# Quantising scales from the maxima alone in a cross-attention and FFN kernel, x normalised by add and multiply, and the instruction orders of all five engines laid anew

## The chip, the cores and the metric

The kernel runs on one NeuronCore of a Trainium2 chip. The core has five engines that run their own instruction streams beside each other: TensorE (PE in the profile), VectorE (DVE), ScalarE (ACT), GpSimd (POOL) and SyncE (SP, which here only issues DMAs). They meet at semaphores alone. The metric is the device time of one launch in microseconds (us), as the median of several runs.

## The reference

One layer of top-k cross-attention, then a feed-forward network whose activations are quantised to 8 bits and whose weights are ternary. All tensors are float32; x is 2048x256, the context 1601x256.

```python
def act_quant(x):
    scale = 127.0 / jnp.clip(jnp.max(jnp.abs(x), axis=-1, keepdims=True), 1e-05)
    q = jnp.clip(jnp.round(x * scale), -128.0, 127.0) / scale
    return x + jax.lax.stop_gradient(q - x)

def bitlinear(x, w, b):
    xq = act_quant(rmsnorm(x))
    wq = weight_quant(w)
    return jnp.einsum('bsd,fd->bsf', xq, wq) + b

# attention: q, k, v projected; scores = q k^T / 16; only the 32 largest
# scores of a row are kept (top_k = 32 of 1601); softmax, times v, projected by Wo
x = x + attention(layernorm(x), ctx)
# FFN: 256 -> 1024 -> 256
h = gelu(bitlinear(layernorm(x), w1, b1))
x = x + bitlinear(h, w2, b2)
```

`rmsnorm(x)` is `x * rsqrt(mean(x*x) + 1e-5)`. A row's maximum after rmsnorm is the row's maximum before it times that row's inverse spread r, so in `round(x * r * 127 / max(x * r))` the r cancels, except where the clip at 1e-5 holds. It is left in the factor that takes the integer back.

## The kernel before

**Tiles.** The 2048 rows are 16 tiles of 128 rows, and two tiles are a pair (8 pairs, `j = t // 2`). Set-up turns the context (13 blocks of 128 rows), folds Wq into Wk and Wo into Wv (`fold_queries`, `fold_values`), and projects the keys in four chunks of 400 or 401 columns (`project_keys`) and the values block by block (`project_values`). Scores need float32 accuracy, so each such product is made of high and low parts, three matmuls for one.

**One tile t.** PE: `scores(t, c)` for four chunks, six matmuls each. ACT: `copy_scores` to `s_sb`. DVE: `candidates` (the 8 largest of each piece of 50), `best_8` and three `next_8` (the 32nd largest of all), `count`, `weigh` (mask times exponentials), `largest_count` and `release(t)`, which raises `p_ready`. ACT: `exp_all(t)` after `best_8(t, 0)`. PE after `release(t)`: `turn_weights(t, q)`, 13 transposes in four quads through the two PSUM banks TURN; ACT: `take_weights` (`pT`, L1101) copies each quad out; PE: `weighted(t, q)`, 26 matmuls. DVE: `attended`, `moments`, `centre` give x2, its mean and variance, and `cen_max`.

**The FFN of a pair.** POOL: `row_scales_1` makes the scales in seven dependent steps of two columns, with the inverse spread second (power -0.5) and the quantising scale sixth. `quantise_1` makes y1; PE turns it (`turn_y1`), `up` multiplies by w1; ACT `hidden` scales by the seventh value; POOL `add_bias`; ACT `gelu` and `squares` (the sums for the second spread); DVE `gelu_max`. POOL `row_scales_2` then waits for squares and maxima, seven steps again; ACT `quantise_2` and `lower_2`; SP turns y2 by DMA, PE `down`, DVE `output`, SP `store`. The last two pairs turn y2 on PE (`turn_y2`), and the last pair makes its scales on DVE tile by tile (`tile_scales_1`, `tile_scales_2`, L1530 to L1534, four steps in front of the quantising), with the power -0.5 on POOL (`root_1`, `root_2`).

**Order.** No scheduler and no pool is in play. Each engine's order is the order in which its calls are written: a set-up by hand, a loop over rounds r in which every stage stands at a fixed offset, and an end by hand. PSUM banks are handed out by `fill` in PE's written order, to the bank of a group that was filled longest ago, so PE waits for whoever has still to drain it. `s_sb`, `e_all` and `pT` have two copies: `copy_scores(t)` waits for `release(t - 2)`.

**Around the change.** `normalise_scale` and `normalise` (L755 to L764, POOL) make xn = (x - mean) * r, `split_queries` (L770) the low part of q, for which `scores` waits. `sum_weights` (L1077, ACT) sums the absolute FFN weights and waits for the DMAs of both w1 and w2. `hold_clock(23)` is 23 transposes whose result nobody reads. The lines that make x normal and the first scale are

```python
pool.tensor_scalar(xn[:, u, :], x_in[:, u, :], ln1_mv[:, u, 0:1], ln1_r[:, 1, u:u + 1],
                   ALU.subtract, ALU.mult)
```

## Time and profile before

| | us |
|---|---|
| median of 3 runs | 279.48 (278.39 to 279.64) |
| span of the profiled execution, first to last instruction | 277.2 |
| PE busy | 262.5 (95%) |
| DVE busy | 230.2 (83%) |
| ACT busy | 215.8 (78%) |
| POOL busy | 165.0 (60%) |

Only the span of the profiled execution is given, not a time with what lies around it. Busy time of PE is modelled from overlapping matmuls: one matmul of `weighted` lasts 0.38 us by itself, while they start 0.22 us apart. So the idle time of PE is what is to be read, and it is spread thinly.

### The profile page before, as it was taken

The numbers are of one execution on the slowest core, as the hardware profiler recorded it, in microseconds if no ns is written. First come the engines' busy times: TensorE is split into PE (matmuls) and PEld (weight loads), VectorE is DVE, ScalarE is ACT, GpSimd is POOL, SyncE is SP. The second block draws the span as 40 slices with busy tenths as digits, with TensorE's granted clock in tenths as the row PEclk, the third lists the DMA queues.
The fourth block names the chain that finished last, engine by engine and source line by source line (L and its number), as shares of the span: only waits on it lengthen the run. The fifth ranks groups of instructions, "written<-read, shape, count | busy, mean of one in ns | idle before, by whom it ended". The sixth has DMA issues, their size and how long they took to land. (4 is left out here: it accounts for less than half of the span.)

```text
span 277.2 us, 5366 instructions
## 1 busy us (share of the span) xinstructions
PE 262.5 (95%) x1527; PEld 230.4 (83%) x1527; DVE 230.2 (83%) x984; ACT 215.8 (78%) x323; POOL 165.0 (60%) x235
## 2 busy tenths in 40 slices
PE   7999999999999899999999999999999999799784
PEld 7999998998887788988898889888978898577463
DVE  2561868988979897989898989899989798989894
ACT  2567495586589988988799879987998899647762
POOL 3334409931888587849775887678767943612330
PEclk9999999999999999999999999999999999999999
DMA  6991010046000330025001500151004100610011
GB/s 223 316 342 40 4 38 0 1 79 151 2 2 0 77 78 0 0 69 125 0 4 45 139 5 4 38 140 18 0 1 124 31 1 2 151 38 5 0 38 38
DMA packets 29436, 16.42 MB, mean 59 GB/s; under 512 B 20445, under 2 KB 28190, under 8 KB 29406
## 3 DMA queue, kind: packets, MB, share of 16 engines
q1 hardware_dynamic: 28702, 15.02, 20.3%
q0 software_dynamic: 272, 0.79, 1.0%
q10 hardware_dynamic: 432, 0.26, 0.3%
q8 instruction: 12, 0.20, 0.3%
q14 instruction: 18, 0.15, 0.2%
HBM read 9.77 MB, written 2.10 MB: 43 GB/s over the span
## 5 line engine op out<-in xcount | busy, mean ns | idle before, releaser
L399 PE MATMUL bank<-vo,pT 128*128 128x257 f32 (+1 forms) x416 | 97.1, 381 | 2.4 <-ACT pT L1101 2.4
L399 PEld LDWEIGHTS bank<-vo,pT 128*128 128x128 f32 (+1 forms) x416 | 76.0, 190 | 15.1 <-ACT pT L1101 4.8
L1413 DVE MAX8 cand<-s_sb 128x8 f32<-128x50 f32 (+1 forms) x512 | 60.0, 201 | 1.6 <-issue 1.1
L258 PE MATMUL score<-k_high,q_low 128*128 128x400 f32 (+1 forms) x128 | 49.5, 387 | 0.0
L868 POOL TENSOR_TENSOR g<-g,b_bc 128x512 f32<-128x512 f32 x24 | 37.9, 1592 | 12.1 <-ACT g L1125 12.1
L258 PE MATMUL score<-k_low,q_high 128*128 128x400 f32 (+1 forms) x128 | 44.2, 346 | 0.0
L258 PE MATMUL score<-k_high,q_high 128*128 128x400 f32 (+1 forms) x128 | 44.0, 344 | 0.0
L1052 ACT ACTIVATE s_sb<-score 128x400 f32<-128x400 f32 x64 | 30.6, 504 | 10.2 <-PE score L258 10.1
L1101 ACT ACTIVATE pT<-bank 128x512 f32<-128x512 f32 x64 | 31.9, 514 | 4.2 <-PE bank L266 4.2
L1448 DVE SCALAR_TENSOR_TENSOR e_all<-s_sb,best,e_all 128x1601 f32<-128x1601 f32 x16 | 34.2, 2138 | 0.9 <-ACT e_all L1093 0.5
L266 PE MATMUL bank<-ident,e_all 128*128 128x128 f32 (+1 forms) x208 | 30.7, 273 | 2.6 <-ACT pT L1101 2.6
L1093 ACT ACTIVATE e_all<-s_sb,neg_max 128x1601 f32<-128x1601 f32 x16 | 26.1, 1629 | 4.5 <-DVE neg_max L1426 4.5
L266 PEld LDWEIGHTS bank<-ident,e_all 128*128 128x128 f32 (+1 forms) x208 | 24.4, 140 | 5.6 <-issue 3.6
L764 POOL TENSOR_SCALAR xn<-x_in,ln_mv,ln_r 128x256 f32<-128x256 f32 x16 | 27.8, 1741 | 0.9
L258 PEld LDWEIGHTS score<-k_high,q_low 128*128 128x128 f32 x128 | 24.1, 189 | 2.4
L258 PEld LDWEIGHTS score<-k_low,q_high 128*128 128x128 f32 x128 | 24.2, 189 | 0.7
L258 PEld LDWEIGHTS score<-k_high,q_high 128*128 128x128 f32 x128 | 24.1, 189 | 0.0
L1609 DVE TENSOR_REDUCE g_max<-g 128x1 f32<-128x1024 f32 x14 | 17.0, 1218 | 7.6 <-ACT g L1135 7.6
L1423 DVE MAX8 best<-cand 128x8 f32<-128x64 f32 (+1 forms) x64 | 20.8, 325 | 2.0
L822 POOL TENSOR_SCALAR row<-ln_mv 128x2 f32<-128x2 f32 x7 | 1.3, 192 | 28.8 <-issue 15.4
L1135 ACT ACTIVATE g<-g 128x1024 f32<-128x1024 f32 x14 | 14.9, 1067 | 3.7 <-POOL g L868 3.7
L1125 ACT ACTIVATE g<-bank,row 128x512 f32<-128x512 f32 x24 | 15.8, 685 | 2.3 <-PE bank L430 2.1
(162 smaller groups left out, 503.2 us busy)
## 6 DMA issues: line engine op xcount, KB each, us to landing
x_in<-in_x SPq DMA_DIRECT2D x16, 128.0 KB, 2.2
w_sb<-in_L_ffn_w SPq DMA_DIRECT2D x2, 1024.0 KB, 12.1
x_res<-in_x SPq DMA_DIRECT2D x16, 128.0 KB, 2.9
out<-o_sb SPq DMA_DIRECT2D x16, 128.0 KB, 2.0
ctx_sb<-in_ctx SPq DMA_DIRECT2D x2, 512.0 KB, 7.6
ctx_sb<-in_ctx SPq DMA_DIRECT2D x2, 256.0 KB, 4.1
b_bc<-in_L_ffn_b POOLq DMA_DIRECT2D x1, 512.0 KB, 7.6
w_q<-in_L_xattn_Wq SPq DMA_DIRECT2D x1, 256.0 KB, 2.8
```

Of the source, the lines that this page charges most:

```text
L258: ins = pe.matmul(out, a, b, start=(i == 0), stop=(i == len(steps) - 1))
L266: ins = pe.transpose(bank[0:src.shape[1], at:at + rows], src, ident[0:rows, 0:rows])
L399: ins = pe.matmul(bank[:, 0:DV], pT[0:n, t % 2, b * P:(b + 1) * P], vo[0:n, b, :], start=(b == 0), stop=(b == SB - 1))
L764: pool.tensor_scalar(xn[:, u, :], x_in[:, u, :], ln1_mv[:, u, 0:1], ln1_r[:, 1, u:u + 1], ALU.subtract, ALU.mult).then_inc(xn_ready, 1)
L868: pool.tensor_tensor(g[:, t % 2, part], g[:, t % 2, part], b1_bc[:, part], ALU.add).then_inc(biased, 1)
L1052: act.activation(s_sb[:, t % 2, at:at + n], score[c][:, 0:n], ACT.Copy).then_inc(s_copied, 1)
L1093: act.activation(e_all[:, t % 2, :], s_sb[:, t % 2, :], ACT.Exp, bias=neg_max[:, t % 2:t % 2 + 1], scale=SCALE).then_inc(e_ready, 1)
L1101: drain(act.activation(pT[0:rows, t % 2, lo * P:hi * P], bank(("p", t, q))[0:rows, 0:(hi - lo) * P], ACT.Copy), ("p", t, q))
L1413: ins = dve.max(cand[:, t % 2, k:CAND:PIECES], s_sb[:, t % 2, k * PIECE:end])
L1423: dve.max(best[:, u, k, :], cand[:, u, 0:DEPTH[k] * PIECES]).then_inc(topk_step[u], 1)
L1448: dve.scalar_tensor_tensor(e_all[:, u, :], s_sb[:, u, :], least_kept(t), e_all[:, u, :], ALU.is_ge, ALU.mult).then_inc(masked, 1)
L1609: dve.tensor_reduce(g_max[:, t % 2:t % 2 + 1], g[:, t % 2, :], AX.X, ALU.max, apply_absolute_value=True).then_inc(g_max_ready, 1)
```

## The change

1. **Scales from the maxima alone.** The quantising scale is now 127 over the maximum, in two steps (`scales_1`, `scales_2` on POOL), with clips 1e-5 * EPS and 1e-5 * EPS ** 0.5 in place of 1e-5. The spread, its power -0.5 and the factor back are four steps of their own (`dequant_1`, `dequant_2`), placed elsewhere in the order. `quantise_1` and `quantise_2` wait for the first two steps. `scales_2` waits for the maxima and no more for `squares`. In the last pair `tile_scales_1` is two steps and `tile_scales_2` three on DVE.
2. **x normalised by add and multiply.** The mean is negated first (one more step of two columns) and then added.
3. **Orders.** The loops are gone; every engine has one written list of the same calls. `sum_weights(0)` and `(1)` stand in front of the last key copies on ACT, `weight_mean` in front of the first scores on PE, and `hold_clock(23)` behind the last matmul.

```diff
-                pool.tensor_scalar(xn[:, u, :], x_in[:, u, :], ln1_mv[:, u, 0:1], ln1_r[:, 1, u:u + 1],
-                                   ALU.subtract, ALU.mult).then_inc(xn_ready, 1)
+                pool.tensor_scalar(xn[:, u, :], x_in[:, u, :], ln1_r[:, 2, u:u + 1], ln1_r[:, 1, u:u + 1],
+                                   ALU.add, ALU.mult).then_inc(xn_ready, 1)
...
-            def row_scales_1(j):
+            def scales_1(j):
...
-                shifted, r, z, step_size, inverse, sc, dq = (row1[:, v, k, :] for k in range(7))
-                step(pool.tensor_scalar(shifted, ln2_mv[:, pair, 1], 1.0 + EPS, EPS * EPS, ALU.mult, ALU.add))
-                step(pool.tensor_tensor(r, shifted, minus_half[:, :], ALU.pow))
-                step(pool.tensor_tensor(z, r, cen_max[:, pair], ALU.mult))
-                step(pool.tensor_scalar(step_size, z, 1e-5, 1.0 / 127.0, ALU.max, ALU.mult))
-                step(pool.tensor_tensor(inverse, step_size, minus_one[:, :], ALU.pow))
-                step(pool.tensor_tensor(sc, inverse, r, ALU.mult))
-                pool.tensor_scalar(dq, step_size, wmean[:, 0:1], None, ALU.mult).then_inc(row1_step, 1)
+                pool.tensor_scalar(row1[:, v, 0, :], cen_max[:, pair], CLIP1, 1.0 / 127.0, ALU.max,
+                                   ALU.mult).then_inc(row1_step, 1)
+                pool.wait_ge(row1_step, base + 1)
+                pool.tensor_tensor(row1[:, v, 1, :], row1[:, v, 0, :], minus_one[:, :], ALU.pow).then_inc(row1_step, 1)
...
             def quantise_2(t):
...
-                act.wait_ge(row2_step, j * ROW2 + 6)
+                act.wait_ge(row2_step, j * ROW2 + 2)
...
             down(13)
-            hold_clock(23)
             turn_y2(14, 0)
             turn_y2(14, 1)
             turn_y2(15, 0)
             turn_y2(15, 1)
             down(14)
             down(15)
+            hold_clock(23)
```

**How the order moves, first place: ACT in the set-up.** `ctx_high`, `k_high` and `wvo_high` are copies that PE's next products wait for, `w1T,wsum` is `sum_weights`, `vo` the values, `q_high` and `q_full` the queries. Before:

```order
L1033 ACTIVATE k_high<-bank,k_bias 128x400
L1003 ACTIVATE bvo_bc<-bank 128x256
L1003 ACTIVATE vo<-bank 128x2x256
L1043 ACTIVATE q_high<-bank,ones 128x512
L1044 ACTIVATE q_full<-bank,ones 128x512
L1077 ACTIVATE w1T,wsum<-w_sb 128x2048
L1033 ACTIVATE k_high<-bank,k_bias 128x401
L1052 ACTIVATE s_sb<-score 128x400
L1033 ACTIVATE k_high<-bank,k_bias 128x401
```

After:

```order
L1231 ACTIVATE k_high<-bank,k_bias 128x400
L1222 ACTIVATE ctx_high<-bank 128x2x65
L1276 ACTIVATE w1T,wsum<-w_sb 128x2048
L1231 ACTIVATE k_high<-bank,k_bias 128x400
L1201 ACTIVATE bvo_bc<-bank 128x256
L1231 ACTIVATE k_high<-bank,k_bias 128x400
L1276 ACTIVATE w1T,wsum<-w_sb 128x2048
L1201 ACTIVATE vo<-bank 128x2x256
L1231 ACTIVATE k_high<-bank,k_bias 128x401 x2
```

Both sums have moved ahead of key copies: the first ahead of four, and the second ahead of the last two.

**Second place: ACT towards the end**, after `exp_all(14)`. `y_raised` and `y` are `quantise_2` and `lower_2` of tiles 10 and 11, `pT` of 128x512 a quad of tile 14, `s_sb` a chunk of scores of tile 15. Before:

```order
L1161 ACTIVATE y_raised<-g,magic_col,row 128x1024
L1179 ACTIVATE y<-y_raised,unmagic_col 128x1024
L1052 ACTIVATE s_sb<-score 128x401
L1161 ACTIVATE y_raised<-g,magic_col,row 128x1024
L1179 ACTIVATE y<-y_raised,unmagic_col 128x1024
L1101 ACTIVATE pT<-bank 128x512 x2
L1093 ACTIVATE e_all<-s_sb,neg_max 128x1601
```

After:

```order
L1362 ACTIVATE y_raised<-g,magic_col,row 128x1024
L1301 ACTIVATE pT<-bank 128x512
L1250 ACTIVATE s_sb<-score 128x401
L1301 ACTIVATE pT<-bank 128x512
L1380 ACTIVATE y<-y_raised,unmagic_col 128x1024
L1354 ACTIVATE g_sq,g_ssq<-g 128x1024
L1301 ACTIVATE pT<-bank 128x512
L1293 ACTIVATE e_all<-s_sb,neg_max 128x1601
```

The copies of tile 14's quads have moved ahead of `lower_2(11)`, and a `squares` has moved in behind it.

**Third place: DVE at the very end**, from `hidden(15, 1)` (`s_sb<-score,row,b_bc`) on. `y_raised` is a half of the last quantising, `g_max` a maximum of half a tile. Before:

```order
L1584 SCALAR_TENSOR_TENSOR s_sb<-score,row,b_bc 128x512 x2
L1564 TENSOR_SCALAR row<-g_ssq 128x1
L1632 SCALAR_TENSOR_TENSOR o_sb<-score,row,x2b 128x256
L1592 TENSOR_REDUCE g_max<-s_sb 128x1
L1530 SCALAR_TENSOR_TENSOR row<-g_max,row 128x1
L1531 TENSOR_SCALAR row<-row 128x1
L1532 RECIPROCAL row<-row 128x1
L1533 TENSOR_TENSOR row<-row 128x1
L1534 TENSOR_SCALAR row<-row,wmean 128x1
L1564 TENSOR_SCALAR row<-g_ssq 128x1
L1592 TENSOR_REDUCE g_max<-s_sb 128x1
L1601 TENSOR_SCALAR y_raised<-s_sb,row 128x512
```

After:

```order
L1928 SCALAR_TENSOR_TENSOR s_sb<-score,row,b_bc 128x512
L1945 TENSOR_SCALAR y_raised<-s_sb,row 128x512
L1936 TENSOR_REDUCE g_max<-s_sb 128x1 x2
L1894 TENSOR_SCALAR row<-g_max 128x1
L1897 TENSOR_SCALAR row<-row 128x1
L1899 RECIPROCAL row<-row 128x1
L1906 TENSOR_SCALAR row<-g_ssq 128x1
L1945 TENSOR_SCALAR y_raised<-s_sb,row 128x512
L1976 SCALAR_TENSOR_TENSOR o_sb<-score,row,x2b 128x256
```

The step that waits for the squares (`row<-g_ssq`) stood ahead of the last maximum and now stands behind the scale, tile 14's scales are done before this stretch, and `output(13)` has gone behind the last quantising.

## Rows read from the trace of the kernel before

**Rows 1.** The page, part 1: busy us, share of span, instructions.
```profile
PE 262.5 (95%) x1527; PEld 230.4 (83%) x1527; DVE 230.2 (83%) x984; ACT 215.8 (78%) x323; POOL 165.0 (60%) x235
```

**Rows 2.** Windows: stretch, its us, busy us of PE, PEld, DVE, ACT, POOL, PEclk, DMA.
```profile
0.00:27.50 27.50, 25.93 (x156) 24.98 (x157) 12.00 (x30) 14.42 (x26) 10.34 (x24) 1.00 0.70 232
27.50:50.00 22.50, 22.50 (x147) 21.58 (x146) 18.03 (x103) 15.00 (x26) 11.46 (x10) 1.00 0.05 13
50.00:230.00 180.00, 176.37 (x994) 154.35 (x993) 161.25 (x728) 155.75 (x228) 129.78 (x174) 1.00 0.19 44
230.00:257.00 27.00, 24.42 (x138) 19.74 (x137) 23.22 (x82) 18.87 (x28) 8.94 (x21) 1.00 0.20 50
257.00:277.20 20.20, 13.28 (x100) 9.76 (x97) 15.67 (x43) 11.78 (x18) 4.49 (x8) 0.99 0.08 26
```

**Rows 3.** Waits of PE: line waited, for whom, us, times, longest.
```profile
PE bank L266 <- ACT pT L1101: 3.3, 5, 1.7
PE bank L399 <- ACT pT L1101: 2.4, 5, 0.6
```

**Rows 4.** Timelines of the set-up: start, us, engine, line, operation [idle before].
```profile
6.56 3.13 SPq L662 DMA_DIRECT2D w_sb<-in_L_ffn_w  x1
25.33 1.92 ACT L1077 ACTIVATE w1T<-w_sb 128x2048 bf16<-128x2048 f32 x1
25.59 1.30 POOL L770 TENSOR_TENSOR q_low<-q_full,q_high 128x512 fp32r<-128x512 f32 x1 [2.05 <-ACT q_full L1044]
27.55 0.34 PE L258 MATMUL score<-k_high,q_low 128*128 128x400 f32 x1
30.42 3.69 DVE L1413 MAX8 cand<-s_sb 128x8 f32<-128x50 f32 x32
```

**Rows 5.** The tile w_sb: from issue to landing of its two DMAs.
```profile
DMA to landing us min/median/max: 10.4/12.1/13.8
```

**Rows 6.** Costliest groups: count, busy us, mean ns, idle before.
```profile
L764 POOL TENSOR_SCALAR xn<-x_in,ln_mv,ln_r 128x256 f32<-128x256 f32 x16 | 27.8, 1741 | 0.9
L835 POOL TENSOR_SCALAR y<-cen,row 128x256 f32<-128x256 f32 x14 | 6.5, 479 | 0.7
L1609 DVE TENSOR_REDUCE g_max<-g 128x1 f32<-128x1024 f32 x14 | 17.0, 1218 | 7.6 <-ACT g L1135 7.6
L1161 ACT ACTIVATE y_raised<-g,magic_col,row 128x1024 f32<-128x1024 f32 x14 | 17.3, 1242 | 0.2 <-POOL row L890 0.2
```

**Rows 7.** Timelines of ACT and PE around 237 us.
```profile
235.28 1.23 ACT L1161 ACTIVATE y_raised<-g,magic_col,row 128x1024 f32<-128x1024 f32 x1
236.54 1.15 ACT L1179 ACTIVATE y<-y_raised,unmagic_col 128x1024 bf16<-128x1024 f32 x1
237.60 1.06 ACT L1101 ACTIVATE pT<-bank 128x512 f32<-128x512 f32 x2
238.32 0.63 PE L266 MATMUL bank<-ident,e_all 128*128 128x128 f32 x4 [1.72 <-ACT pT L1101]
```

**Rows 8.** Timeline of DVE behind the last attention product.
```profile
257.05 0.17 DVE L1497 RECIPROCAL inv_sum<-bank 128x1 f32<-128x1 f32 x1 [0.72 <-PE bank L399]
264.71 1.40 DVE L1584 SCALAR_TENSOR_TENSOR s_sb<-score,row,b_bc 128x512 f32<-128x512 f32 x2
268.09 0.67 DVE L1592 TENSOR_REDUCE g_max<-s_sb 128x1 f32<-128x512 f32 x1
269.08 0.69 DVE L1530 SCALAR_TENSOR_TENSOR row<-g_max,row 128x1 f32<-128x1 f32 x1
```

**Rows 9.** Timelines of ACT and PE in the same stretch, and PE's first matmuls.
```profile
266.81 1.06 ACT L1153 ACTIVATE g_sq<-s_sb 128x1024 bf16<-128x1024 f32 x1
270.48 0.82 ACT L1170 ACTIVATE y_raised<-s_sb,magic_col,row 128x512 f32<-128x512 f32 x1 [1.77 <-DVE row L1533]
265.57 2.67 PE L420 MATMUL bank<-ident 128*128 128x128 f32 x23
271.35 1.09 PE L266 MATMUL score<-ident,y_raised 128*128 128x128 f32 x8 [1.47 <-ACT y_raised L1170]
1.52 4.95 PE L462 MATMUL score<-ident 128*128 128x128 f32 x22 [1.52 <-POOL ident L739]
```

More of the change, by code:

```diff
@@ L557, in _ @@
+            down(9)
+            turn_weights(13, 2)
+            weighted(13, 0)
             turn_weights(13, 3)
@@ L945, in _ @@
             quantise_1(2, 1)
[L946 to L976 removed]
+            dequant_1(2)
@@ new lines, in _ @@
+            copy_scores(13, 0)
+            hidden(8, 1)
+            take_weights(11, 0)
+            hidden(9, 0)
+            take_weights(11, 1)
+            copy_scores(13, 1)
+            hidden(9, 1)
+            gelu(8)
+            gelu(9)
+            exp_all(12)
+            take_weights(11, 2)
+            take_weights(11, 3)
+            quantise_2(8)
+            copy_scores(13, 2)
+            lower_2(8)
+            take_weights(12, 0)
+            squares(8)
+            take_weights(12, 1)
@@ new lines, in _ @@
+            copy_scores(13, 3)
+            take_weights(12, 2)
+            squares(9)
+            quantise_2(9)
+            take_weights(12, 3)
+            take_queries(7)
+            exp_all(13)
+            lower_2(9)
+            take_y1(5)
+            copy_scores(14, 0)
+            hidden(10, 0)
+            copy_scores(14, 1)
+            hidden(10, 1)
+            copy_scores(14, 2)
+            hidden(11, 0)
+            copy_scores(14, 3)
+            hidden(11, 1)
+            gelu(10)
@@ L1740, in _ @@
             count(13)
+            output(8)
             attended(12)
```

1331 lines of the change are left out of this document (898 added, 433 removed).

## The prediction, made before the changed kernel had run

> **What bounds the kernel now.** I read the page's first part, then windows by stage, then PE's waits, then timelines where PE idles. PE is busy 262.5 us of 277.2 [rows 1], so its idle time is 14.7 us, and no reordering gives back more than that. The windows say where it lies [rows 2]: 1.6 us up to 27.5, none up to 50, 3.6 in the 180 us from 50 to 230, 2.6 from 230 to 257, and 6.9 in the last 20.2. In the middle the others are close behind: per 180 us DVE is busy 161 and ACT 156. So three engines run at 87 to 98%, and a late copy on ACT or a late mask on DVE reaches PE at once. PE's waits in the attention are all for `pT`, the ACT copies of the turned weights [rows 3]: 3.3 us ahead of transposes and 2.4 ahead of products. The end is another regime: behind the last `weighted` (257.05 [rows 8]) 20.2 us follow in which single steps wait for each other, and of PE's busy time there 2.67 us are `hold_clock` [rows 9].
>
> **Set-up, a loss of 0.7 us for PE and a gain for DVE.** `sum_weights(0)` now stands ahead of the third chunk's key copies. It waits for both FFN weight loads. The second was issued at 6.56 and the slower of the two took 13.8 us [rows 4, 5], so it lands near 20.4; `sum_weights` lasts 1.92, so the first key copy behind it starts near 22.4, while PE, by its own work, has those keys ready near 20.8. Behind it stand two more copies (0.6 each), the second sum (to about 26.2) and `take_values(0)` (to 26.8), which frees the bank that `weight_mean` takes. So the first scores start near 27.0 instead of 27.55 [rows 4]. But PE has less behind it then: `project_values(1)`, 12 matmuls 0.12 apart or 1.4 us, now comes later, `weight_mean` (0.14) earlier. 27.55 - 1.3 = 26.3 would be no loss, so 27.0 is a loss of 0.7. POOL is a second candidate for last: `join_biases` waits for the bias copy (to about 23.5), then 0.7, two `normalise`, and the split of 1.30 [rows 4]. With `normalise` at 0.48 that ends at 26.5, with 1.22 at 28.0, and the loss is then 1.7. DVE, in return, no longer has copies of scores ahead of its last key step; `candidates(0)` starts near 28.8, not 30.42.
>
> **Normalising on POOL.** `(subtract, mult)` on 256 columns lasts 1.74 us in the mean, `(mult, add)` on as many 0.48 [rows 6]. `(add, mult)` with two column operands isn't in the trace. Its bounds are these two rows; I take 0.48, since add and multiply are the two operations of the fast row and subtract is the one thing that only the slow row has. That is 16 x 1.26 = 20 us less of POOL, against 8 small steps of 0.2. POOL is busy 60%, and its `normalise` has almost no one waiting for it (the queries are turned rounds ahead), so on PE's path I count nothing for it in the middle, from either bound. The cover is the distance of the queries; if it is gone, one late `normalise` costs 1.2. The Trainium skill ("GPSIMD Engine Reference", 3.1 Elementwise) has every body of up to two operations at 1.03 cycles an element, which makes 256 columns about 0.4 us by an estimate from that page, whatever the operations. The row of 0.48 agrees, the row of 1.74 does not, so the trace and not the page says that subtract is dear.
>
> **Scales from the maxima.** For the first six pairs the quantising scale waits for two POOL steps instead of six, and the second no more for `squares`. `quantise_2` waits 0.2 us for it in 14 instructions today [rows 6]: there is nothing to gain where it stands. What the split buys is freedom of place, and the new order spends it by quantising sooner after the gelu. The dequant steps are out of the way of `quantise_1` but `hidden` waits for them now; between them lie `turn_y1`, its copy and an `up`, over 2 us of work, against four steps of about 1.4 in all. Nothing, then.
>
> **The middle, 50 to 230, a gain of 1.8.** The amount of PE work is the same call by call. Scores of the even tiles stand 8 to 10 us of PE work further ahead of their use, so DVE's candidates have them sooner; DVE idles 7.6 us today in front of `gelu_max` [rows 6]. The bounds are a gain of 3.6 (all of PE's idle time) and the loss of rival 2 below. I take half, 1.8, as new positions remove some of the fixed-offset waits and bring others.
>
> **Towards the end, 230 to 257, a gain of 2.1.** One wait is seen to go. At 236.6 PE wants a bank for the third quad of tile 14 and waits 1.72 until ACT has copied the first; ACT was in `quantise_2(11)` (1.23) and `lower_2(11)` (1.15) first [rows 7]. In the new order both copies are ahead of `lower_2(11)`. DVE also has less in front of `release(15)`: `output(10)`, `output(11)` (0.47 each) and both halves of `hidden(12)` (0.7 each), 2.3 us, have moved behind it. PE in turn has `turn_y1_tile(14)` and `up(14, 0)` ahead of its last product, 0.6 more. Of the 2.6 idle I take back 2.6 + 0.1 from DVE's head start, less 0.6: 2.1.
>
> **The tail, a gain of 1.8.** Before: `hidden(15, 1)` ends at 264.71 + 1.40 = 266.1 [rows 8], the last `y_raised` at 270.48 + 0.82 = 271.3 [rows 9], 5.2 apart. In between the DVE step that waits for the squares (266.81, 1.06 and its read-out) holds the last maximum until 268.09, and a first scale step takes 0.69 [rows 8, 9]. Now: quantise a half (0.42), two maxima (1.27), three small steps (0.55), then ACT's 0.82, together 3.1. That is 2.1 less. Earlier in the tail `hidden(14, 1)` and a maximum are put between `attended(15)` and `quantise_1(15)`, while four small steps and the other half leave it; I make that 0.3 worse. Behind the last `y_raised` nothing changes: 277.2 - 271.35 = 5.85. `hold_clock` at the end runs 2.5 us beside the last output and its store and costs nothing.
>
> **The sum.** 277.2 + 0.7 - 1.8 - 2.1 - 1.8 = 272.2 of span. The median of the runs is 2.3 above the profiled span, and so I add 2.3: 274.5.
>
> **Rival 1: PE's clock falls in the tail.** `hold_clock` filled the gap from 265.57 to 268.2; now PE idles there. I lay PE's tail as about 6 us idle in the 10 before the last transposes, with one gap of 2.4, where before the longest was 1.6 and the clock granted was 0.99 of full in the last stretch [rows 2]. If it falls to the lower level, the last 8 transposes and 16 products of `down` start at the spacing of the first matmuls, 4.95 / 22 = 0.22 apart [rows 9] instead of 0.11: 24 x 0.11 = 2.6, so 277.1. The Trainium skill ("TensorE: Matmul & The Clock Gate", Part 1) says that the throttled state is the default and activity lifts it; by that rule 277.1 is the time if the tail is too idle. The trace shows no fall at gaps of 1.6 and can't decide 2.4.
>
> **Rival 2, slower: ACT stands at `quantise_2` with copies behind it.** In the new order `quantise_2(4)` follows `gelu(5)` after a query copy, `exp_all(8)` and one `take_weights`, about 4.9 us. It needs `gelu_max(4)` and `(5)` (2 x 1.22 [rows 6]) and two POOL steps (1.0). That is 3.5, a margin of 1.4; but on DVE `output(2)` stands first, and waits for `down(2)` on PE. Where this is late, ACT waits with `take_weights` queued behind it, and PE waits for banks. At 1.5 us a pair over six pairs that is 9.0: 283.5. It makes the kernel slower from 0.8 us a pair. For it: ACT has no slack to catch up. Against it: DVE has 10% to spare there, and the scores come earlier.
>
> **Rival 3: the gains cancel.** The middle keeps its waits in other places (+1.8) and the slow `normalise` holds the first scores (+1.0): 277.3. Beside it stands a better case: the middle loses nearly all its idle time, 272.5.
>
> **Chances and range.** My forecast, 272.8 to 276.3, has 0.46. The better case has 0.16, the clock 0.08, cancelled gains 0.13 (its times spread to 279.5), the slower rival 0.17. The range of 8 in 10 reaches from 270.8 to 281.0. A measurement can tell about 0.5% (1.4 us) from no change. Faster than 278.1: 0.74; within 0.5%: 0.11; slower: 0.15.
>
> **What would show it.** `L1161` or `L1170` on ACT waiting for a POOL row by more than 0.2 us in all supports rival 2. POOL's xn group near 480 ns or near 1200 decides the normalise. PE's windows: idle in the middle under 3.6 us, and no wait near 1.7 for `pT` towards the end. Between `hidden(15, 1)` and the last `y_raised` 3.1, not 5.2. The matmuls of the last `down` 0.11 apart or 0.22. The first scores near 27.0. I am wrong at the root if PE's idle time in the middle grows: then written order, not work, sets the time.

## The result, and the profile after

The changed kernel takes 285.17 us in the median of four runs (284.31 to 287.06), the kernel before beside it on the same chip 279.39. The ratio is 1.0228, with a 95% interval from 1.0189 to 1.0268: it is slower by 2.3%, where 274.5 us, faster by 1.7%, had been forecast. The time lies above the range too. The profiled run is 284.93 us long with a span of 283.0, against a span of 277.2 before. All numbers of the profile below are this run's.

The page's first part, as [rows 1]:

```profile
PE 265.4 (94%) x1527; PEld 233.7 (83%) x1527; DVE 230.8 (82%) x978; ACT 214.4 (76%) x323; POOL 150.6 (53%) x229
```

PE issues the same 1527 matmuls. It is busy 2.9 us longer with them and idle 17.6 us instead of 14.7, 2.9 more. The two make the 5.8 us of the span. The windows, with the columns of [rows 2], say where:

```profile
0.00:27.50 27.50, 24.73 (x149) 23.53 (x150) 13.01 (x34) 16.68 (x29) 10.12 (x28) 1.00 0.68 218
27.50:50.00 22.50, 19.10 (x125) 18.82 (x124) 20.21 (x99) 12.44 (x20) 16.33 (x17) 0.93 0.13 42
50.00:230.00 180.00, 175.15 (x980) 153.74 (x979) 152.62 (x691) 145.35 (x217) 102.97 (x150) 0.99 0.19 44
230.00:257.00 27.00, 25.58 (x152) 21.39 (x152) 24.47 (x105) 22.60 (x32) 15.62 (x24) 1.00 0.16 36
257.00:283.00 26.00, 20.79 (x130) 16.25 (x127) 20.45 (x53) 17.28 (x27) 5.53 (x11) 0.93 0.08 26
```

From 27.5 to 50 PE had no idle time at all before. Now it has 3.4 us, and a granted clock of 0.93 in the mean: work is lost there twice. In the stretch behind 257 the clock is 0.93 too. The larger waits of PE from the set-up's contexts on, and the last for `pT` (line, for whom, us in all, times, longest), are of another kind than [rows 3]:

```profile
PE bank L267 <- DVEq L1817: 4.8, 3, 3.4
PE bank L267 <- POOL y L998: 2.3, 2, 1.9
PE score L267 <- ACT y_raised L1371: 2.0, 1, 2.0
PE score L259 <- POOL q_low L926: 2.0, 1, 2.0
PE bank L267 <- DMA ctx_sb<-in_ctx: 1.2, 1, 1.2
PE bank L267 <- ACT pT L1301: 0.4, 1, 0.4
```

The 5.7 us of waits for `pT` (ten of them, one of 1.72 towards the end and nine of 0.6 at most) are down to 0.4. In their place stand a few single waits of 1.1 to 3.4 us, and two of them name POOL, the engine whose work the change had made shorter. The longest is at 41.9, for `release(0)`. The timelines of DVE, POOL and PE there (start, us; of PE two matmuls before the wait, the transposes that waited, and two matmuls of the first shape after it):

```profile
37.55 2.28 DVE L1785 SCALAR_TENSOR_TENSOR cand_ge<-cand,best,cand_worth 128x256 bf16<-128x256 f32 x1
39.76 3.51 DVE L1778 SCALAR_TENSOR_TENSOR e_all<-s_sb,best,e_all 128x1601 f32<-128x1601 f32 x1
...
37.59 1.96 POOL L952 TENSOR_SCALAR w_sb<-w_sb,winv 128x2048 f32<-128x2048 f32 x1
39.64 1.95 POOL L955 TENSOR_SCALAR w_sb<-w_sb 128x2048 f32<-128x2048 f32 x1
41.67 2.72 POOL L926 TENSOR_TENSOR q_low<-q_full,q_high 128x512 fp32r<-128x512 f32 x1
...
41.44 0.28 PE L259 MATMUL bank<-wvo_low,ctx_high 128*128 128x256 f32 x1
41.56 0.28 PE L259 MATMUL bank<-wvo_high,ctx_high 128*128 128x256 f32 x1
...
45.60 1.09 PE L267 MATMUL bank<-ident,e_all 128*128 128x128 f32 x8 [3.40 <-DVEq L1817]
...
48.19 0.41 PE L259 MATMUL bank<-wvo_high,ctx_low 128*128 128x256 f32 x1
48.40 0.42 PE L259 MATMUL bank<-wvo_low,ctx_high 128*128 128x256 f32 x1
```

`cand_ge` of `count(0)` is listed with 2.28 us, and the median of its 16 is 0.485; `e_all` of `weigh(0)` with 3.51, and its median is 1.885. Beside them POOL runs both passes of `ternary(1)`, which stood at 48.4 before, behind the split of the queries. That is 3.4 us late for `release(0)`, as much as the wait. Behind the wait the matmuls start 0.21 us apart instead of 0.12: PE has the lower of its two clock levels (1.2 instead of 2.4 GHz) from 46.9 to 50.3.

Such a meeting is not new, and it does not always cost something. The masks of the kernel before are longer in the mean (2138 ns, with one of 2.69 at 51 and three of 2.97 behind it) than those of the changed kernel (2014 ns), and PE has no wait for a mask. And beside the two passes of `ternary(0)` (kernel before; each 1.9 to 2.0 us) nobody is late: DVE takes maxima of one operand there, 3.69 us long as at 30.42 [rows 4]:

```profile
41.77 1.98 POOL L795 TENSOR_SCALAR w_sb<-w_sb,winv 128x2048 f32<-128x2048 f32 x1 [8.72 <-DVE winv L1406]
42.80 3.69 DVE L1413 MAX8 cand<-s_sb 128x8 f32<-128x50 f32 x32 [1.13 <-issue]
```

The second such place is at 184 (GpSimd, VectorE):

```profile
182.60 0.22 POOL L1039 TENSOR_SCALAR row<-g_max 128x2 f32<-128x2 f32 x1 [3.50 <-DVE g_max L1953]
183.57 2.94 POOL L926 TENSOR_TENSOR q_low<-q_full,q_high 128x512 fp32r<-128x512 f32 x1
183.51 1.87 DVE L1778 SCALAR_TENSOR_TENSOR e_all<-s_sb,best,e_all 128x1601 f32<-128x1601 f32 x1
```

`split_queries(6)` stands behind `scales_2(3)`, which waits for the maxima; then it lasts 2.94 us instead of its median of 1.29, beside a mask that keeps its 1.87. PE waits 2.0 and has the lower clock for 3.4 us again. And the tail:

```profile
274.79 0.81 ACT L1371 ACTIVATE y_raised<-s_sb,magic_col,row 128x512 f32<-128x512 f32 x1 [0.41 <-DVE row L1899]
275.66 1.97 PE L267 MATMUL score<-ident,y_raised 128*128 128x128 f32 x8 [2.01 <-ACT y_raised L1371]
277.42 2.67 PE L455 MATMUL score<-w2T,y2T 128*128 128x256 bf16 x16
279.93 2.67 PE L421 MATMUL bank<-ident 128*128 128x128 f32 x23
```

PE waits 2.01 us, and its last transposes start 0.22 apart. The filler, now at the end, comes when there is nothing left to keep the clock for.

### The profile page after: what moved, and what is told of

It is laid out like the page before. It is cut to its first block, busy times and chain, and to the rows that moved or that the text cites. A ratio compares the mean times of both kernels' runs of the same rounds, so it can differ in the third digit from the quotient of the medians.

```text
span 283.0 us, 5387 instructions
## 1 busy us (share of the span) xinstructions
PE 265.4 (94%) x1527; PEld 233.7 (83%) x1527; DVE 230.8 (82%) x978; ACT 214.4 (76%) x323; POOL 150.6 (53%) x229
## 4 chain that ended last, share of the span: by engine, by line
PE 51%; DVE 15%; POOL 12%; issue 9%; ACT 6%; DMA 4%; SPq 1%; DVEq 1%; POOLq 0%; ACTq 0%
PE bank L400 18%; PE score L259 15%; PE bank L267 8%; PE bank L259 3%; POOL g L1031 3%; DMA ctx_sb<-in_ctx 3%; DVE cand L1743 3%; DVE e_all L1778 3%; DVE g_max L1953 3%; PE bank L431 2%; PE bank L455 2%; POOL q_low L926 1%; POOL y L998 1%; DVE cand_ge L1785 1%; PE score L455 1%
## 5 line engine op out<-in xcount | busy, mean ns | idle before, releaser
L1743 DVE MAX8 cand<-s_sb 128x8 f32<-128x50 f32 (+1 forms) x512 | 61.7, 203 | 7.9 <-issue 4.6
L259 PE MATMUL score<-k_high,q_low 128*128 128x400 f32 (+1 forms) x128 | 50.4, 394 | 2.1 <-POOL q_low L926 2.0
L259 PE MATMUL score<-k_low,q_high 128*128 128x400 f32 (+1 forms) x128 | 44.9, 351 | 0.0
L1031 POOL TENSOR_TENSOR g<-g,b_bc 128x512 f32<-128x512 f32 x24 | 32.0, 1349 | 9.9 <-ACT g L1326 9.9
L267 PE MATMUL bank<-ident,e_all 128*128 128x128 f32 (+1 forms) x208 | 31.6, 277 | 5.4 <-DVEq L1817 4.8
L1778 DVE SCALAR_TENSOR_TENSOR e_all<-s_sb,best,e_all 128x1601 f32<-128x1601 f32 x16 | 32.2, 2014 | 2.0 <-ACT e_all L1293 2.0
L926 POOL TENSOR_TENSOR q_low<-q_full,q_high 128x512 fp32r<-128x512 f32 x8 | 13.9, 1744 | 12.1 <-ACT q_full L1242 12.0
L1009 POOL TENSOR_TENSOR x2b<-x,b_bc 128x256 f32<-128x256 f32 x16 | 11.7, 734 | 15.1 <-DVE x L1829 15.1
L1362 ACT ACTIVATE y_raised<-g,magic_col,row 128x1024 f32<-128x1024 f32 x14 | 17.1, 1240 | 1.6 <-POOL row L1042 1.5
```

What stands on the lines that cost most here:

```text
L259: ins = pe.matmul(out, a, b, start=(i == 0), stop=(i == len(steps) - 1))
L267: ins = pe.transpose(bank[0:src.shape[1], at:at + rows], src, ident[0:rows, 0:rows])
L1031: pool.tensor_tensor(g[:, t % 2, part], g[:, t % 2, part], b1_bc[:, part], ALU.add).then_inc(biased, 1)
L1362: act.activation(y2_raised[:, t % 2, :], g[:, t % 2, :], ACT.Identity, scale=row2[:, j % 2, 1, t % 2:t % 2 + 1], bias=magic_col[:, 0:1]).t ...
L1743: ins = dve.max(cand[:, t % 2, k:CAND:PIECES], s_sb[:, t % 2, k * PIECE:end])
L1778: dve.scalar_tensor_tensor(e_all[:, u, :], s_sb[:, u, :], least_kept(t), e_all[:, u, :], ALU.is_ge, ALU.mult).then_inc(masked, 1)
```

## The experiments

Ratios are to the kernel before, run in turn on the same chip, with 95% intervals. The chips differ by up to 0.5%, so ratios are compared and not medians. All runs compute all that the reference asks for by the same steps as the changed kernel or the one before; d_fill and y_lock add work that nobody reads. The expectations give waits of PE some 0.16 us longer than the profile lists them (3.56 for the 3.40 at 41.9).

**b_ternary**: does GpSimd's `ternary(1)` make VectorE late?

```diff
             ternary(0)
+            ternary(1)
             normalise_scale(2)
...
             normalise(2, 1)
-            ternary(1)
```

> The changed kernel with one edit on GpSimd: ternary(1) stands directly behind ternary(0), as in the kernel before. Nothing else is moved and the same values are computed.
> Theory (single waits caused by GpSimd's work lying beside VectorE's): in the changed kernel ternary(1) runs at 37.6 to 41.6 us, beside count(0) and weigh(0); VectorE's cand_ge of count(0) takes 2.28 us there and weigh(0)'s e_all 3.51 us, release(0) ends late, and TensorE waits 3.56 us at 41.9 and then shows half its clock until 50.3. With ternary(1) away from there, cand_ge should take near 0.5 us and e_all near 1.9 us, the wait at 41.9 should be under 0.5 us and the clock whole from 40 to 50; time 4 to 5 us under the changed kernel (285.2), so 280 to 281.
> Rival (the new order on VectorE and ScalarE holds TensorE up, whatever GpSimd does): release(0) stays where it is within 1 us and the time within 1 us of 285.2.
> Second rival (ternary(1) moved ahead puts off the splits of the queries or the first normalised pairs, and a wait of the same size stands elsewhere): the wait at 41.9 goes, another of 2 us or more comes between 20 and 40 us, and the time stays within 2 us of 285.2.

Measured: 1.0157 (1.0090 to 1.0224), span 280.4. VectorE, and the first and the new waits of PE:

```profile
37.58 0.47 DVE L1785 SCALAR_TENSOR_TENSOR cand_ge<-cand,best,cand_worth 128x256 bf16<-128x256 f32 x1
37.98 1.88 DVE L1778 SCALAR_TENSOR_TENSOR e_all<-s_sb,best,e_all 128x1601 f32<-128x1601 f32 x1
...
PE bank L267 <- DVEq L1817: 3.6, 3, 2.3
...
PE score L259 <- ACT s_sb L1250: 1.3, 1, 1.3
```

Both VectorE passes have their usual length, the wait at 41.9 is gone and the clock is whole from 40 to 50. So the cause of that wait is shown. But the waits are not fewer: the 3.4 us come back as 3.6 in two others that were hidden behind it, 1.3 at 51 for a copy of scores behind `lower_weights(1)` and 2.3 at 68 for `release(2)`, and PE is idle 5.8 us from 28 to 100 in both kernels. What is gone from the span, 2.6 us, is the lower clock's part (1.6, from d_fill's rows below) and 0.8 of the wait for contexts in the set-up (1.17 before, 0.35 now), which this edit doesn't touch. The median (283.2) missed the 280 to 281 expected, and the two intervals overlap. The second rival was right in kind, only that the new waits stand behind 50 and not before 40: the order has no room there.

**d_fill**: what does the lower clock cost by itself? 30 useless transposes inside the wait for `release(0)`, 18 inside that for `q_low`.

```diff
+                if (t, q) == (0, 0):
+                    bank = fill(("p", t, q), TURN)
+                    for _ in range(30):
+                        pe.transpose(bank[:, 0:P], ident[:, :], ident[:, :])
+                    pe.wait_ge(p_ready, t + 1)
...
```

> The changed kernel with useless transposes on TensorE inside its two longest waits: 30 into the bank of turn_weights(0, 0) ahead of its wait for release(0), 18 ahead of the wait of scores(12, 0) for q_low. What is waited for is not touched, and the same values are computed.
> Theory (a wait costs twice, once as itself and once by the clock that TensorE is granted behind it): the clock at 40 to 50 and 180 to 190, which reads 0.84 in the changed kernel, reads 1.0; release(0) and q_low come when they came; the time falls by the clock's part alone, 2.5 to 3.5 us, to 282 to 283.
> Rival (the lower clock behind the waits costs nothing, since the other engines set the pace there): the clock is whole and the time within 1 us of 285.2.

Measured: 1.0058 (1.0028 to 1.0088). Windows of PE (us, busy, clock, DMA):

```profile
40.00:50.00 10.00, 9.87 (x83) 1.00 0.10 27
180.00:190.00 10.00, 9.97 (x60) 1.00 0.18 42
270.00:280.00 10.00, 7.69 (x54) 0.83 0.12 41
```

The first two rows read 0.84 in the changed kernel. What was waited for came when it had come, and the same work behind it is done sooner. The first transposes of `e_all` and the scores that follow, in d_fill:

```profile
45.56 0.66 PE L394 MATMUL bank<-ident,e_all 128*128 128x128 f32 x4
48.72 0.43 PE L259 MATMUL score<-k_high,q_low 128*128 128x400 f32 x1
```

They stand 3.16 us apart, and 4.73 in the changed kernel (45.60 and 50.33), so one fall of 3.4 us costs 1.6, and the two 3.1. By the ratios 4.7 us are saved, more than the 2.5 to 3.5 expected. By the profiled runs, both with the fall in the tail, it is 2.0 of span, since 1.4 us come back in a wait for `release(2)` at 69.5: the rival, that others set the pace, holds for that part. How often the clock falls also differs from run to run of one kernel. One fall takes 0.006 off the mean granted clock (half of 3.4 us in 283). The changed kernel's four runs have 0.982, 0.982, 0.982 and 0.970; five of d_fill's ten have 1.00, so no fall even in the tail, and are the faster for it (spans of 277.4 to 279.2, the others 279.0 to 281.3). So 2.0 to 4.7 of the 6.4 us (2.28%) by which the changed kernel is slower are this second price of waits.

**c_split**: would the queries be in time with another row on GpSimd?

```diff
             residual(10)
+            split_queries(6)
             scales_2(3)
-            split_queries(6)
```

> The changed kernel with one edit on GpSimd: split_queries(6) ahead of scales_2(3) instead of behind it, as in no other place. The same values are computed.
> Theory (a queue on GpSimd): scores(12, 0) waits 2.14 us for q_low, because split_queries(6) stands behind scales_2(3), which waits for g_max until 183.6, and then runs beside weigh(10) for 2.94 us; after it TensorE shows half its clock for 3.4 us. Moved ahead, q_low is there some 1.5 us or more before scores(12, 0) asks, the wait and the clock's fall go, and the time falls by 2 to 3.7 us, to 281.5 to 283. Scales_2(3) comes no later, for g_max binds it.
> Rival (ScalarE is late: take_queries(6) ends only at 182.2): split_queries(6) can't start before 182.2 whatever stands ahead of it, the wait shrinks by 1 us at most and the clock falls all the same; time within 1 us of 285.2.

Measured: 1.0237 (1.0180 to 1.0294), nothing gained. GpSimd, VectorE and ScalarE:

```profile
182.94 1.27 POOL L926 TENSOR_TENSOR q_low<-q_full,q_high 128x512 fp32r<-128x512 f32 x1 [4.14 <-ACT q_full L1242]
184.18 1.79 POOL L1039 TENSOR_SCALAR row<-g_max 128x2 f32<-128x2 f32 x1
183.21 2.68 DVE L1778 SCALAR_TENSOR_TENSOR e_all<-s_sb,best,e_all 128x1601 f32<-128x1601 f32 x1
186.79 1.24 ACT L1362 ACTIVATE y_raised<-g,magic_col,row 128x1024 f32<-128x1024 f32 x1 [3.93 <-POOL row L1042]
```

My theory fell. `q_low` is early now, but the mask behind it takes 2.68, and then an instruction of GpSimd on two numbers a lane, 0.22 us long elsewhere, takes 1.79, until the mask has ended. The scale is 3.1 us later, ScalarE stands at `quantise_2(6)`, the copy of scores behind it is late, and PE waits 2.2 for that. Here rival 2 of the prediction is seen at work, made by an experiment.

**a_hold**: the filler back in the tail.

```diff
             down(13)
+            hold_clock(23)
             turn_y2(14, 0)
...
             down(15)
-            hold_clock(23)
```

> The changed kernel with one edit on TensorE: the 23 useless transposes of hold_clock stand between down(13) and turn_y2(14, 0) again, as in the kernel before, not at the program's end. The same values are computed.
> Theory (the clock in the tail): the changed kernel waits 2.18 us at 273.4 and has half the clock from 275.5 to 279.0, in which the last transposes and products run, worth about 1.7 us. With the filler back the clock is whole up to the end. The filler itself lies in waits of 0.8 to 1.3 us and puts later work off by 0 to 1 us. Time 0.7 to 1.7 us under 285.2, so 283.5 to 284.5.
> Rival (the filler is in the way: it takes 2.5 us, and the waits it may fill are shorter now): time 0 to 1 us above 285.2, with the clock whole.
> Second rival (the filler ends too far ahead of the wait at 273.4): clock falls as before and the time stays or rises.

Measured: 1.0163 (1.0093 to 1.0233), span 280.0, clock 1.00 from 270 to the end. It agrees with the theory, and the interval is too wide for the size: the four runs have mean clocks of 0.994, 0.988, 0.982 and 0.976 and take 281.8, 282.3, 284.7 and 286.0 us in this order, and the profiled one is the fastest. Of its 3.0 us of span 1.6 are the clock's fall at 184, which this profiled run doesn't have though its wait is the same; the tail's own part is 1.4.

**e_norm, h_sub, f_scales**: the operations without the order, and the reverse. e_norm is the kernel before with add and multiply; f_scales has all of the change's operations, and each engine's order as before; h_sub is the changed kernel with the old subtraction:

```diff
-                pool.tensor_scalar(xn[:, u, :], x_in[:, u, :], ln1_r[:, 2, u:u + 1], ln1_r[:, 1, u:u + 1],
-                                   ALU.add, ALU.mult).then_inc(xn_ready, 1)
+                pool.tensor_scalar(xn[:, u, :], x_in[:, u, :], ln1_mv[:, u, 0:1], ln1_r[:, 1, u:u + 1],
+                                   ALU.subtract, ALU.mult).then_inc(xn_ready, 1)
```

> The kernel before with one edit: x is normalised by add and multiply, with the negated mean from one more short instruction of GpSimd for each pair. Orders and scales as before.
> Theory (a faster GpSimd off the critical path is worth nothing by itself): the rows of xn take near 0.55 us instead of 1.74, GpSimd's busy time falls by some 15 to 20 us, and the time stays within 0.5% of the kernel before (278.2 to 280.9).
> Rival (GpSimd's queue holds TensorE up in the kernel before): 1.5 us or more faster.

> The changed kernel with the old form of the normalisation, x minus mean times root, in place of add and multiply. Nothing else is changed, so the extra negated mean is computed and not used.
> Theory (the form of the instruction alone sets its length, and it hides in GpSimd's idle time but for the first pairs): the rows of xn take 1.2 to 1.7 us again, GpSimd is busy some 15 to 20 us more; the time is the same or up to 1.5 us over the changed kernel's 285.2.
> Rival (the new order leans on the short form): 287 or more.

> The kernel before with all new operations of the change and none of its new order: scales from the maxima alone (two short steps ahead of the quantisation, the four of the later factor behind it), x normalised by add and multiply, and every engine's order as before; on VectorE's last pairs each factor stands directly ahead of its first user. The same values are computed as in the changed kernel.
> Theory (the operations are good or neutral, the new order is what costs): the normalised rows take near 0.55 us instead of 1.2 to 1.7, quantisation finds its scale 1 to 3 us earlier, TensorE's regular waits stay near those of the kernel before; time at or under the kernel before, 277.5 to 279.5.
> Rival (the new operations cost, by more steps on GpSimd or later factors that hidden(t) waits for): 281 or more, near the changed kernel.

Measured: e_norm 0.9998 (0.9983 to 1.0012); h_sub 1.0226 (1.0190 to 1.0261), by its ratio no different from the changed kernel; f_scales 0.9917 (0.9898 to 0.9935). Its repetition on another chip:

> The kernel of f_scales once more, word for word: the kernel before's order with the change's new operations. Theory and rival alike: 276.5 to 277.8, by 0.7 to 1% under the kernel before.

gave 0.9923 (0.9897 to 0.9949). **So the new operations make the kernel faster by 0.8%, and the new order makes it slower by 3.1%.** In the old order the normalisation has no part in it. In the new order that is not settled: in h_sub PE waits 1.37 us for `q_low` and the first scores start at 28.41 instead of 26.96, and its two runs at the changed kernel's usual clock of 0.982 have spans of 285.3 and 285.9 (282.5 to 283.6 there, and chips differ by 0.3 us here), while its two others have fewer falls of the clock (0.988 and 0.994; spans 283.1 and 283.5). Its rows (shortest, median and longest in ns) in the kernel before, e_norm, h_sub and f_scales:

```profile
L764 POOL TENSOR_SCALAR xn<-x_in,ln_mv,ln_r x16: 1204/1230/2898, 19.4 to 203.2; 128x256 f32<-128x256 f32 x16
...
L765 POOL TENSOR_SCALAR xn<-x_in,ln_r x16: 543/551/2202, 19.4 to 203.2; 128x256 f32<-128x256 f32 x16
...
L920 POOL TENSOR_SCALAR xn<-x_in,ln_mv,ln_r x16: 1215/1230/1472, 14.6 to 190.7; 128x256 f32<-128x256 f32 x16
...
L766 POOL TENSOR_SCALAR xn<-x_in,ln_r x16: 541/548/557, 19.6 to 201.8; 128x256 f32<-128x256 f32 x16
```

The form with the subtraction costs 1.23 us and the one with the addition 0.55 (the column that it reads is another one too). It is no rule for all subtractions: `q_low`, a subtraction of two tensors of 128x512, takes 1.27 us at its shortest, as does the addition of that shape in y_lock. In e_norm GpSimd is busy 11 us less, not the 15 to 20 expected, as four of the short rows still take 2.2. The mean of 1741 in [rows 6] is a mixture: five of the sixteen were near 2.9 in the kernel before, each starting beside a mask of VectorE. That answer was to be had before the prediction, and would have shown the mechanism that this change met.

**g_all**: every large wait mended by a move of one or two places.

> The changed kernel with each of its large waits mended by a move of one or two places: ternary(1) behind ternary(0) on GpSimd; weigh(2) directly behind count(2) and weigh(14) behind count(14) on VectorE; lower_weights(1) behind take_values(6) on ScalarE; take_queries(6) ahead of exp_all(10) on ScalarE and split_queries(6) ahead of scales_2(3) on GpSimd; on TensorE fold_key_bias ahead of turn_context(2), turn_y1(0) behind weighted(2, 3), and the filler of hold_clock ahead of turn_y2(14, 0) as in the kernel before. The same values are computed.
> Theory (the new order loses only in a few single places, and its gains in the middle are real): of TensorE's 25 us of waits some 10 go (1.3 at 8.5, 3.6 at 41.9, 2.0 at 82, 2.1 at 184, 1.2 at 242) and 3 to 5 us of half clock besides; what lies behind them gives part of it back. Time 272 to 276, under the kernel before (279.5).
> Rival (the waits are the slack of VectorE's and ScalarE's queues: mended in one place they come in the next, as half of it did with ternary(1) alone): 278 to 281.

Measured: 1.0107 (1.0082 to 1.0132), 282.7 us. The rival was right in kind, and the time lies above its range too. The waits for masks are as long in all as in the changed kernel, in five pieces:

```profile
PE bank L267 <- DVEq L1817: 4.9, 5, 1.7
PE bank L267 <- POOL y L998: 2.0, 3, 1.4
```

The clock is whole (1.00) in this run and one more, but four of the six have 0.986 to 0.994: no wait over 1.8 us is left in the profile, and that alone doesn't keep the clock. The early place of `fold_key_bias` was worth nothing: PE waits 0.8 for the copy of the bias instead.

**Crosses of the two orders.** Each engine follows one order up to a task and the other for what is left. The diffs only move lines.

> A cross of two orders with the changed kernel's operations: every engine follows the changed kernel's order up to about 100 us (TensorE up to down(0), ScalarE up to lower_2(1), VectorE up to count(5), GpSimd up to quantise_1(1, 1)) and the kernel before's order from there, filler in the tail included. The same values are computed.
> Theory (the new order loses in the first 100 us): TensorE's waits there sum to 9.7 us in the changed kernel against 3.3 with the old order and the same operations (the run f_scales, 277.1 us), and half clock from 46.9 to 50.3 adds 1.6. The cross should take 277.1 + 6.4 + 1.6, so 283 to 285.
> Rival (the loss comes from the middle or the tail, and the first part is made good later): 277 to 280.

Measured: 1.0269 (1.0217 to 1.0322), 286.6 us: at least the whole loss, and more than the 283 to 285 expected.

> A cross with the changed kernel's operations: its order of the set-up on every engine (TensorE up to weight_mean, ScalarE up to the copies of scores(0), VectorE up to candidates(0), GpSimd up to ternary(0), the queue of SyncE up to the third load of x), the kernel before's order from there. The same values are computed.
> Theory (the set-up costs what the prediction gave it, 0.7 us or a little more, and the loss of the first part stands between 28 and 100 us, where GpSimd's and VectorE's work lie beside each other): f_scales (277.1) + 0.5 to 1.5, so 277.5 to 278.7; candidates(0) start near 30 instead of 27.
> Rival (the later start of candidates(0) and the new queue of transfers are what the whole first part loses): 281 or more.

Measured: 0.9939 (0.9916 to 0.9963), 0.64 us over f_again, and not told from none, as the intervals overlap. With l_head (the ratios differ by 3.3%, 9 us, of which a wait of 1.1 at 104 belongs to the place where the orders meet): the set-up costs 0.6, and the stretch from 28 to 100 us some 8. The rows name 6 of the 8: from 28 to 100 PE is idle 5.8 us in the changed kernel and 1.5 in f_scales, and the fall of the clock is 1.6.

> The opposite cross: new operations, the kernel before's order up to about 232 us and the changed kernel's order of the tasks that are left from there (TensorE from turn_weights(13, 0), ScalarE from take_weights(13, 1), VectorE from count(14), GpSimd from the biases of tile 10), with the filler of hold_clock ahead of turn_y2(14, 0) as in the kernel before. The same values are computed.
> Theory (the new tail is worth what the prediction gave it): attended(15) no later than in f_scales, and 1.3 to 2 us less from there to the end; clock whole; 275 to 276.5, against 277.1 of f_scales.
> Rival (the new order on VectorE, which puts weigh(14) behind two pieces of candidates(15), holds turn_weights(14, 0) up, and the tail gives back no more than that costs): 277 to 279.

Measured: 0.9967 (0.9943 to 0.9992), 278.25 us, in the rival's range. It settles nothing, since where the orders meet PE waits 3.1 us for a bank (up to 229.7, for `output(8)`), a fault of the cross.

> New operations, the kernel before's order up to about 100 us and the changed kernel's order of the rest, with three of its waits mended (take_queries(6) ahead of exp_all(10) and split_queries(6) ahead of scales_2(3); weigh(14) ahead of candidates(15, 0); the filler ahead of turn_y2(14, 0)). The same values are computed.
> Theory (the new order's middle and tail are as good as or better than the old one's): waits from 100 us on were 12.9 us in g_all and 11.9 in f_scales, of which 2.5 at 186 to 199 came from what the mended queue pushed back; 276 to 278.5.
> Rival (the new middle costs too): 279 to 281.

Measured: 1.0231 (1.0192 to 1.0270). The 276 to 278.5 us expected were missed by far (285.7), and so was the rival's 279 to 281. But this too has faults of its own where the orders meet: waits of 1.8 and 2.7 at 103 and 109, and one of 3.0 at 241 for a mask. Whether the new middle costs anything stays open.

> The kernel before's order with the new operations up to about 240 us, the changed kernel's order from there (TensorE from turn_weights(14, 0), ScalarE from lower_2(11), VectorE from output(10), GpSimd's last few), filler in the tail as before. The same values are computed.
> Theory (the tail's step of the prediction is right in kind): ScalarE's lower_2(11) no longer stands ahead of take_weights(14, 1), so the wait of 1.9 us at 235.5 shrinks to near 0.7, and from attended(15) to the end 1.3 us or more are saved; 274.5 to 276, which would be the fastest of all.
> Rival (what the order gives ahead of attended(15) it takes after, since the same work stands on VectorE in another row): 276.6 to 278.

Measured: 0.9898 (0.9873 to 0.9923), 275.92 us, the fastest kernel; beside f_again (276.40) the gain of the tail's order is 0.5 us and not told from none. Its trace shows two parts. The wait at 235.5 is down from 1.72 to 0.45, but PE then waits for `release(15)`:

```profile
246.56 1.09 PE L267 MATMUL bank<-ident,e_all 128*128 128x128 f32 x8 [1.63 <-DVEq L1817]
267.24 0.81 ACT L1371 ACTIVATE y_raised<-s_sb,magic_col,row 128x512 f32<-128x512 f32 x1 [0.40 <-DVE row L1899]
```

and from `attended(15)` (256.6) to the end of the last `y_raised` (268.05) are 11.4 us, where the kernel before has 14.25.

**y_lock**: does the meeting itself set the length, and who waits?

```diff
+                if r == 2:
+                    idle_adds(10, 1, 3)
                 if live(r + 5):
                     normalise(r + 5, 1)
+                if r == 1:
+                    idle_adds(8, 0, 1)
```

> The kernel of f_scales with useless additions of GpSimd (128x512, like those of the bias, which take 1.28 us alone) in its idle time: one behind normalise(6, 1), which starts after VectorE's weigh(8) has started, and two behind count(10), which start just ahead of weigh(10). They are written to a buffer that nobody reads; all that the reference asks for is computed.
> Theory (an instruction of GpSimd and a pass of VectorE over two operands in SBUF exclude each other, and the one that came second waits): the one at 145.7 is listed with 2.5 to 3 us (it waits for e_all to end and takes 1.28 then), and weigh(8)'s e_all keeps near 1.9; of the two at 173 the first takes near 1.3 and weigh(10)'s e_all is listed with 1 to 2.6 us more than its 1.88.
> Rival (they share the memory port and both get slower by some tens of per cent while they overlap): both the additions and e_all rise to 1.5 to 2.5 us, none by the whole length of the other.
> The time: by either within 1 us of f_scales, 276.2 to 278.2, since release(10) has some slack.

Measured: 0.9988 (0.9968 to 1.0007), by the ratios 1.8 us over f_again. The additions came one pair later than I had counted, behind `weigh(10)` and ahead of `weigh(12)`:

```profile
173.99 2.88 POOL L809 TENSOR_TENSOR junk<-b_bc 128x512 f32<-128x512 f32 x1
173.85 1.89 DVE L1482 SCALAR_TENSOR_TENSOR e_all<-s_sb,best,e_all 128x1601 f32<-128x1601 f32 x1
...
201.93 4.10 POOL L809 TENSOR_TENSOR junk<-b_bc 128x512 f32<-128x512 f32 x2
202.33 2.55 DVE L1482 SCALAR_TENSOR_TENSOR e_all<-s_sb,best,e_all 128x1601 f32<-128x1601 f32 x1
```

At 174 the mask was there first: it keeps its 1.89, and the addition, 1.27 at its shortest, is listed with 2.88, which is what is left of the mask and then its own length. At 202 the first addition was first: the mask waits for it (2.55, which is 0.67 more and not the 1 to 2.6 expected, as only 0.9 of the addition was left) and the second addition for the mask. Whoever comes second waits, by about the other's remainder. The rival, both slower by a share, is out. The Trainium skill says as much ("SBUF — State Buffer", SBUF: two separate sides): the pair of ports that the two engines share is an exclusive lock, held for the whole instruction by whichever starts first, against VectorE's instructions in a two-port mode or with two SBUF inputs, the latter only where the GpSimd instruction reads SBUF. The traces agree, with the sizes above. Three useless additions in idle time of GpSimd cost 1.8 us in the end, so the time expected (within 1 us) was missed.

## Why the prediction was wrong, by its own steps

- **What bounds the kernel.** Right, and its warning was the result: with three engines at 87 to 98%, a late mask on DVE reaches PE at once. The view of 27.5 to 50, no idle time at all, gave no term of the sum, so the stretch was put at nothing without a reason. That, with the gain booked for the middle, was the step that failed. The change moves `ternary(1)` there, 4 us of POOL, and new DVE tasks, and I priced neither: +3.4 us of idle time, and a clock at half for 3.4 us, worth 1.6. `ternary(1)` is not the whole of it: without it 3.6 us of other waits come up to 70 us (b_ternary), so it is the new order of several engines that is late there. To ask only what waits for a moved instruction is too little; it is to be asked as well what runs beside it.
- **Set-up, +0.7.** u_setup gives 0.6 for the whole set-up, which is not told from none. The first scores start at 26.96 as laid (27.0), and so does the key copy behind `sum_weights(0)`, at 22.54 (22.4). But `candidates(0)` starts at 30.07 and not 28.8, for DVE waits 3.2 us for a load of x that `ln1_stats(2)` needs, and PE waits 1.2 for the contexts that `turn_context(2)` was moved up to (0.35 in b_ternary, with the same order).
- **Normalising, 0.48 us, worth nothing.** It takes 0.55 and is worth nothing in the old order (e_norm). The slow form's price in the set-up was laid rightly too: first scores at 28.0, and 28.41 in h_sub. The bound of 1.74 was no price of subtraction, as said above; subtraction is 1.23.
- **Scales from the maxima, 0.** Where it stands in the middle it is worth little: PE's idle time from 50 to 230 is 3.2 us in f_scales and 3.6 before. Its worth is in the tail, where I had booked it, so far as it can be placed. From `attended(15)` to the last `y_raised` f_again takes 13.1 us, the kernel before 14.25, m_tail 11.4: 1.1 us by the operations, 1.7 by the order. The rest of the 2.0 us of span that f_scales gains is not placed.
- **The middle, -1.8.** The wrong sign: +1.3 of idle time, and 1.6 for the clock's fall at 187. The waits for `pT` there went, 3.5 us down to 0.4, as that step hoped. But 1.9 for `y1` at 82 and 2.0 for `q_low` at 184 came, both behind an instruction of POOL that VectorE's mask held up, and idle time in the middle is 4.9 us instead of 3.6.
- **Towards the end, -2.1.** The wait of 1.72 is gone, as predicted. From 230 to 257 idle time is 1.4 instead of 2.6, so 1.2 of it came; a wait for `release(14)` of 1.1 stands in the same stretch.
- **The tail, -1.8.** `hidden(15, 1)` ends at 272.5, the last `y_raised` at 275.6: 3.1, as predicted. From `attended(15)` to there 11.4 us instead of 14.25. Then rival 1 took 1.5 back (7.4 us from there to the end, 5.9 before). PE's idle time behind 257 is 5.2 us and was 6.9.
- **Rival 1**, the clock, had a chance of 0.08, and happened in three places. The price was right in kind, 2.6 for 24 instructions, and 1.5 in fact: the clock came back after 3.4 us. The chance was wrong. I had asked it of the tail alone, while it can fall behind any long wait.
- **Rival 2** had the right sign for the wrong reason. `quantise_2` waits 1.5 us in 14 instructions, not 9 us; where it would have happened, c_split shows. The loss came from late masks and splits, some of them by two engines that exclude each other, and from the clock behind them; the first of these no rival held. The last line of the prediction, that written order and not work sets the time if PE's idle time in the middle grows, is what happened.

What is shown by taking it away: the wait at 41.9 and its cause (b_ternary), the price of the clock (d_fill), that operations and order have opposite signs (f_scales), that the set-up is small (u_setup) and the normalisation in the old order nothing (e_norm). Argued from rows alone: that the wait for `y1` at 82 is the same exclusion. Open: why the new orders need 4.3 us more of PE's waiting from 28 to 100 us. What b_ternary and c_split took away came back as waits elsewhere, of what g_all took away much did (4.5 us idle from 28 to 100), and no run crosses single engines.

## What to carry to other kernels

Before moving a long GpSimd instruction, lay it on VectorE's timeline and not only on its own queue: beside a VectorE pass over two SBUF operands both take turns, and the one that comes second is late by the other's rest. Look at shortest, median and longest of a group, never at its mean alone; where the longest of one shape is twice the median, look for a meeting. It costs only where somebody waits for the late one, so look too at what is queued behind it: a wait that is taken away can come back whole at the next task. And where PE is the bound, many waits of 0.5 us are cheaper than one of 2 to 3.5, since behind the long one it may run at half its clock for 3.4 us, 1.6 us each time here; a filler belongs inside the wait.

## What was not expected of the hardware

- An instruction of GpSimd on two numbers a lane took 1.79 us instead of 0.22, as it started while a mask of VectorE ran.
- TensorE's granted clock fell to its lower level behind waits of 3.4, 2.0 and 2.0 us in the changed kernel, each time for 3.4 us, and in the crosses behind 2.7, 3.0 and 3.1. It did not fall behind the same 2.0 at 184 in b_ternary and a_hold, behind 2.3 at 68 in b_ternary, nor behind 2.2 at 189 in c_split; but in u_setup it fell in the set-up, where two waits of 0.4 and 1.2 stand 3 us apart. The length of one wait alone doesn't decide it, and one kernel has a different number of falls in different runs.
- A subtraction of one operand and a column on VectorE (`cen`, 128x256, median 0.35 us) is held up by GpSimd too: 1.18 us in y_lock, at 175.85 and at 205.00, each time beside the end of an addition.
